# Second maximum and second exponentials moved directly behind the first, and a block's layer-norm steps behind the maxima

## What is computed

```python
def attention(x, w_kv_down, w_kv_up, w_q, w_out):
    kv = (x @ w_kv_down) @ w_kv_up
    k, v = kv[..., :HD], kv[..., HD:]                 # 16 heads of 64
    q = x @ w_q
    att = einsum('bqhd,bkhd->bhqk', q, k) * 64 ** -0.5
    att = softmax(where(causal, att, -inf), axis=-1)
    return einsum('bhqk,bkhd->bqhd', att, v).reshape(B, T, HD) @ w_out

def ffn(x, centroids, gamma, beta, W1, b1, W2, b2):
    expert = argmax(feats @ centroids.T, axis=1)
    alpha = sigmoid(sum(feats * centroids[expert], axis=-1))
    h = layernorm(feats) * gamma[e] + beta[e]
    y = feats + relu(h @ W1[e].T + b1[e]) @ W2[e].T + b2[e]     # e = expert of the token
    return alpha * y + (1 - alpha) * feats

x = x + layernorm(attention(layernorm(x)))
x = x + layernorm(ffn(layernorm(x)))
```

## Time and profile before

| | us |
|---|---|
| timed runs, median (lowest to highest) | 1460.65 (1459.31 to 1461.14) |
| the profiled execution, its own time | 1459.58 |
| span of its trace | 1457.7 |
| TensorE / VectorE / ScalarE / GpSimd busy, share of the span | 92% / 85% / 74% / 56% |
| the attention's steady part, 30 to 1235 us: TensorE busy | 1146.59 of 1205 |
| one iteration (16 slots) in the steady part | 75.88 |
| mean granted TensorE clock (1 is full) | 0.977 |

### The profile page before, as it was taken

How to read it: one execution, slowest core, us unless ns; L and a number is a source line. 1 busy time by engine, 2 the same in 40 slices (tenths; PEclk the granted TensorE clock), 3 DMA queues, 4 the chain that set the end, 5 groups by cost and what they waited for, 6 DMA issues and landing times.

```text
span 1457.7 us, 34718 instructions
## 1 busy us (share of the span) xinstructions
PE 1343.0 (92%) x9120; PEld 1210.6 (83%) x9120; DVE 1234.4 (85%) x4806; ACT 1083.2 (74%) x3186; POOL 809.8 (56%) x1216
## 2 busy tenths in 40 slices
PE   7999999999999999999999999999999999599993
PEld 6988898888888988888888888888888888488872
DVE  5899888888888888888888888888888887499994
ACT  5888787878787878788787878787878886366661
POOL 3445555555555555555555555555555554178886
PEclk9999999999999999999999999999999999699997
DMA  4000000000000000000000000000000000312120
GB/s 194 5 9 12 12 11 12 11 8 11 12 11 12 11 11 10 9 11 11 11 11 12 11 10 11 10 11 12 11 12 11 9 9 14 95 48 63 59 62 8
DMA packets 38793, 32.39 MB, mean 22 GB/s; under 512 B 4882, under 2 KB 35990, under 8 KB 38304
## 3 DMA queue, kind: packets, MB, share of 16 engines
q1 hardware_dynamic: 31968, 21.61, 4.9%
q0 software_dynamic: 4608, 8.67, 1.7%
q10 hardware_dynamic: 2112, 1.11, 0.3%
HBM read 20.35 MB, written 12.07 MB: 22 GB/s over the span
## 4 chain that ended last, share of the span: by engine, by line
DVE 46%; issue 22%; ACT 18%; POOL 6%; PE 5%; ACTq 1%; DMA 1%; DVEq 1%; POOLq 0%; SPq 0%
DVE nscore L851 15%; DVE p_lo L861 13%; ACT prob L722 10%; ACT t_hi L694 5%; DVE nmax L851 2%; POOL prob L1037 2%; DVE ff L367 2%; DVE hitr L891 2%; DVE wup_s L384 1%; DVE on L393 1%; POOL pay L1056 1%; DVE fn L793 1%; DVE gg L402 1%; DVE t_lo L838 1%; DVE rinv L832 1%
## 5 line engine op out<-in xcount | busy, mean ns | idle before, releaser
L1037 POOL TENSOR_TENSOR prob<-prob,rinv 128x256 f32<-128x256 f32 (+1 forms) x512 | 413.2, 828 | 507.8 <-DVE rinv L832 507.7
L722 ACT ACTIVATE prob<-nscore,nmax 128x128 f32<-128x128 f32 (+1 forms) x1024 | 458.7, 449 | 248.4 <-DVE nmax L851 248.4
L851 DVE CUSTOM_DVE_ANT_0 nscore<-psS,mask 128x128 f32<-128x128 f32 (+1 forms) x1024 | 319.9, 350 | 0.0
L861 DVE TENSOR_TENSOR p_lo<-psP,p_hi 128x768 fp32r<-128x768 f32 x256 | 243.7, 952 | 1.0 <-ACT p_hi L694 0.9
L838 DVE TENSOR_TENSOR t_lo<-psT,t_hi 128x512 fp32r<-128x512 f32 x256 | 175.9, 687 | 56.0 <-ACT t_hi L694 56.0
L607 PE MATMUL psP<-ident,prob 128*128 128x128 f32 x1536 | 216.4, 277 | 6.8 <-DVE p_lo L861 6.7
L694 ACT ACTIVATE p_hi<-psP 128x768 fp32r<-128x768 f32 x256 | 204.9, 800 | 1.6 <-PE psP L607 1.6
L579 PE MATMUL psS<-t_lo,xt_hi 128*128 128x256 f32 (+1 forms) x512 | 196.8, 384 | 0.0
L722 ACT ACTIVATION_READ_ACCUMULATOR prob<-nscore,nmax 128x1 f32 x1024 | 191.3, 187 | 0.0
L607 PEld LDWEIGHTS psP<-ident,prob 128*128 128x128 f32 x1536 | 167.2, 141 | 22.7 <-POOL prob L1037 8.8
L867 DVE TENSOR_TENSOR z_lo<-psZU,z_hi 128x512 fp32r<-128x512 f32 x256 | 175.7, 686 | 3.3 <-ACT z_hi L694 3.3
(11 more groups left out here) (167 smaller groups left out, 3246.0 us busy)
## 6 DMA issues: line engine op xcount, KB each, us to landing
fin<-routed_rows SPq DMA_DIRECT2D x40, 136.0 KB, 2.2
wx<-ffn_w SPq DMA_DIRECT2D x2, 2058.0 KB, 12.0
xin<-x SPq DMA_DIRECT2D x32, 128.0 KB, 2.1
xres<-x SPq DMA_DIRECT2D x32, 128.0 KB, 2.1
out<-res,fin POOLq DMA_INDIRECT x80, 2.3
routed_rows<-padr ACTq DMA_DIRECT2D x4, 272.0 KB, 4.3
routed_rows<-padr SPq DMA_DIRECT2D x4, 272.0 KB, 5.4
wup_s<-wup SPq DMA_DIRECT2D x1, 1024.0 KB, 4.9
```

The costliest lines, as they stand in the source:

```text
L722: last = nc.scalar.activation(prob[:, p1, h, a:z], nscore[:, h, a:z], ACT.Exp, bias=nmax[:, p1, h, q:q + 1], scale=-1.0, accum_out=rsum[:, ...
L851: last = v.tensor_tensor_reduce(nscore[:, h, a:z], psQ[q][:, h, :], mask[:, a:z], -1.0, -MASKED, ALU.add, ALU.min, nmax[:, p1, h, q:q + 1])
L861: v.tensor_tensor(p_lo[:, (s - 3) % 2], psP[:, :, 0:384], p_hi[:, (s - 3) % 2].bitcast(F32), ALU.subtract).then_inc(S["p_split"], 1)
L1037: last = g.tensor_tensor(pr, pr, rinv[:, p2, :, q:q + 1].broadcast_to([P, 2, z - a]), ALU.mult)
```

## The change

Three things move; no arithmetic is added or taken away.

1. On VectorE `score_max(1)` stands directly behind `score_max(0)` and ahead of `p_lo` (in r = 4 the routing's step 3 stays between them, its step 4 follows them). On ScalarE `exps(1)` stands directly behind `exps(0)` and ahead of `z_hi`.
2. The layer-norm steps of r = 0 to 3 leave the head of the slot. `block_norms` (`an`; `st3`; `fn` and `st1`; the writes and `xn`) stands behind both maxima and ahead of `p_lo`; `block_moments` (`mv3`, `mv1`) stands between `p_lo` and `z_lo`.
3. On GpSimd the chain of six linked steps in r = 1 is cut: the two that make the reciprocal deviation stay in r = 1 (with two semaphores of their own, `ve3_done` and `rs3_done`, on which `fn` waits), the other four move to r = 2, behind that slot's product with `rinv`.

```diff
             # ScalarE
                 if live(1):
                     exps(0)
+                    exps(1)
                 if live(4):
...
                     cp(z_hi[:, (s - 4) % 2], psZ[:]).then_inc(S["z_hi_done"], 1)
-                if live(1):
-                    exps(1)
             # VectorE
                 if live(1):
                     score_max(0)
                 route(b0, s, live_b, 3)
+                if live(1):
+                    score_max(1)
                 route(b0, s, live_b, 4)
+                block_norms(b0, s, live_b)
                 if live(3):
                     dve.wait_ge(S["p_hi_done"], g0 + s - 2)
                     v.tensor_tensor(p_lo[:, (s - 3) % 2], psP[:, :, 0:384], p_hi[:, (s - 3) % 2].bitcast(F32),
                                     ALU.subtract).then_inc(S["p_split"], 1)
-                if live(1):
-                    score_max(1)
+                block_moments(b0, s, live_b)
                 if live(4):
                     dve.wait_ge(S["z_hi_done"], g0 + s - 3)
...
-            def misc_stats(b0, s, live_b):
+            def block_moments(b0, s, live_b):
...
                 if r == 1 and live_b(2):
                     aggregate(st3, mv3, S["st3_done"], S["mv3_done"], b0 + db - 1)
                 if r == 2 and live_b(-1):
                     aggregate(st1, mv1, S["st1_done"], S["mv1_done"], b0 + db + 2)
+
+            def misc_stats(b0, s, live_b):
...
                 if r == 2 and live_b(2):
-                    n = b0 + db - 1
-                    dve.wait_ge(S["r3_steps"], 6 * n - 4)
+                    dve.wait_ge(S["rs3_done"], n)
                     normalise(lambda t: fn[:, t, :], lambda t: pay[:, db, t, 0:P], mv3,
                               lambda t: pay[:, db, t, C_RSTD:C_RSTD + 1], S["f_ready"])
             # GpSimd
                 if r == 1 and live_b(2):
+                    inv_sqrt(pay[:, db, :, C_RSTD], ve3, mv3[:, :, 1], S["mv3_done"], S["ve3_done"], S["rs3_done"],
+                             b0 + db - 1)
+                if r == 2 and live_b(2):
                     n = b0 + db - 2
-                    k = [6 * n]
+                    k = [4 * n]
...
-                    pool.wait_ge(S["mv3_done"], n + 1)
-                    link(g.tensor_tensor(ve3[:], mv3[:, :, 1], eps_t[:], ALU.add))
-                    link(g.tensor_tensor(rs3, ve3[:], neg_half[:], ALU.pow))
-
+                    pool.wait_ge(S["rs3_done"], n + 1)
                     link(g.tensor_tensor(w3[:, 0, :], mv3[:, :, 1], rs3, ALU.mult))
```

More of the change, by code:

```diff
@@ L149, in block_kernel @@
             bias_done bias_added weights_ready
-            x_loaded xr_loaded st1_done mv1_done ve1_done rs1_done xn_ready xk_hi_done xn_tr xt_hi_done x_split xk_split
+            x_loaded xr_loaded ve3_done rs3_done st1_done mv1_done ve1_done rs1_done xn_ready xk_hi_done xn_tr xt_hi_done x_split xk_split
             t_ready t_hi_done t_split s_ready nmax_ready probs_ready rinv_ready norm_ready pt_ready p_hi_done p_split
@@ L925, in misc_stats, with block_norms @@
                     aggregate(st1, mv1, S["st1_done"], S["mv1_done"], b0 + db + 2)
+            def misc_stats(b0, s, live_b):
+                r, db = s % PAIRS, s // PAIRS
                 if r == 7 and live_b(1):
                     aggregate(st2, mv2, S["st2_done"], S["mv2_done"], b0 + db)
-            def misc(g0, b0, s, live, live_b):
+            def block_norms(b0, s, live_b):
                 r, db = s % PAIRS, s // PAIRS
+                n = b0 + db - 1
                 if r == 0 and live_b(2):
-                    n = b0 + db - 1
                     dve.wait_ge(S["rs2_done"], n)
@@ L962, in misc @@
                     prep_norm((db + 1) % 2, b0 + db + 2, b0 + db + 1)
+            def misc(g0, b0, s, live, live_b):
+                r, db = s % PAIRS, s // PAIRS
+                if not live(0) and s == 9:
+                    dve.wait_ge(S["bias_done"], E // 2 + 1)
+                    b1v = wx[:, :, B1:W2]
+                    v.tensor_tensor(b1v, psT[:, 0, 0:E * FB].rearrange("p (e j) -> p e j", e=E), b1v,
+                                    ALU.add).then_inc(S["bias_added"], 1)
                 if r == 6 and live_b(-1):
```

## The result

The changed kernel takes 1491.39 us (median of four runs, 1490.78 to 1493.51), against 1459.98 for the kernel before beside it: a ratio of 1.0215, with a 95% interval of 1.0199 to 1.0232, or 31.4 us slower. The forecast was slower, but by 9, and its range ended at 1479.

What follows compares the result with a forecast made beforehand. It took a 4.31 us slot cycle through two engines as the bound, TensorE close behind at 4.23. Blocks -5.6, boundary +5.3 and clock +9.6 summed to +9.3 on 1459.58, or 1470.0 on the median; range 1457 to 1479.

Steps and rivals of the forecast that it cites:

- plain slots: Attention slots without extra steps: the new cycle through `z_lo` was to take 4.22 us in place of 4.31.
- the straight line through two points: Loop boundary: TensorE waits of 1.1 us never drop the clock, 2.09 did in 4 of 13; 2.99 gives 8 of 13.
- the block walk: One block of eight slots, r = 0 to 7, summed to 36.79 us against 36.97; over 31 blocks -5.6 us.
- five small routing steps: Slot r = 5, from `z_lo` to first maximum: 1.63 us with these steps, against 1.30 plain.
- rival (c): GpSimd's product with `rinv` holds the moved `fn` and `xn`: 8.4 us; 1469 without the clock, 1478 with it; chance 0.10.
- the slots of r = 5 to 7: Sign that the forecast is right: these slots longer than before, and slot 4 shorter by 0.6 us.
- The boundary, +5.3: Loop's branch: 2.35 us in a cycle without spare time, where it cost 1.94; 13 times 0.41.
- The clock, +9.6: TensorE idling at the boundary: 8 falls to half clock at 1.45 us each, in place of 4 at 0.5.
- My upper bound on the price, 1.7: Clock fall behind a boundary: 3.4 us at half clock loses at most 1.7 us of work; 1.45 was taken.
- Part 3, at nothing: GpSimd's cut chain in r = 1 and 2: product (1.61 us) and moved steps (about 2.5) fill a slot; costed at nothing.

## Why the prediction failed

**The direction and three of the mechanisms were right.** The second exponentials follow the first; `z_lo` waits for `z_hi`; plain slots take 4.19 (forecast 4.22); `z_lo` to the first instruction behind the branch takes 2.99 (2.95). The clock falls behind 8 of 13 boundaries, which is the number given, and an iteration with one stretch is 1.3 to 1.4 longer than without (1.45 given). The products added at the boundary show that it is the falls that cost this, and that without TensorE's idling there they don't come. The number itself owes something to luck: the straight line through two points that gave it is not what the other runs show, with eight boundaries also at 6.7 to 7.0, and six at 7.3 to 7.4.

**The step that failed is the block walk, -5.6 us, measured +10.2.** Most of it, 11.2, is the cast: I priced the "five small routing steps" of r = 5 at their times from the kernel before, where GpSimd's product had ended when the cast came. The change doesn't move it among VectorE's instructions, so it was in no list of moved steps; but it comes 1.32 behind `rinv` in place of 1.85, and the product runs from 0.24 to 1.85 behind `rinv`. I had weighed that hold, but as rival (c) for `fn` and `xn` alone. These two were not held. GpSimd and VectorE in r = 2 of the changed kernel:

```profile
329.69 1.61 POOL L1045 TENSOR_TENSOR prob<-prob,rinv 128x256 f32<-128x256 f32 x2
```

```profile
331.33 0.60 DVE L792 TENSOR_SCALAR fn<-pay,mv 128x128 f32<-128x128 f32 x2
```

`fn` starts 0.03 us behind the product's end and takes its 0.60, as in the earlier trace rows. So these rows say nothing on whether the product could hold it. The mechanism was right and the instruction was not. The Trainium skill (SBUF — State Buffer, Who interferes with whom) lists a cast among the operations that can take the port shared with GpSimd, and says that a tensor_tensor with both inputs in SBUF contends with GpSimd's reads; the rows of the cast (0.56 against 0.16) and of `hitr` (0.81 against 0.175) agree with both.

The other 4.6 are in the walk itself: without the held cast the block takes 36.94 and not 36.79. The walk reaches the first maximum of r = 4 after 18.59, and measured are 18.78; behind that, the cast left out, it is 0.05 too long. The kernel with `an` behind `p_lo` puts 0.3 us a block on `an` ahead of `p_lo`, in r = 1 and 2. I had taken it on the path once, and let TensorE's pace cover it from then on; one block walked once from r = 0 can't show what a late start leaves in the next slots. That the slots of r = 5 to 7 would be longer than before was right for r = 6 (4.87 for 4.31), right for r = 5 by the held cast alone (4.89 for 4.65, and 4.52 with the cast late), and wrong for r = 7 (4.18 for 4.31).

**The boundary, +5.3, measured +7.0.** The place and the mechanism were as given; 2.48 for 2.35.

**The clock, +9.6, measured +12.9 in the twelve iterations, and 14.3 with the fall behind them.** The count was right; the price was not, since four of the eight boundaries have two stretches in a row, at 2.7 us. My upper bound on the price, 1.7, excluded that. The doubled stretches went when `an` was late, which brings the transposes nearer, but also when the cast was late, which leaves the boundary as it is; why, no run shows.

**Part 3, at nothing**: no run takes GpSimd's chain back alone, so that is not shown; in the changed kernel VectorE waits 1.6 us in all for that chain, ahead of `fn`, and 1.7 before.

**What stays open.** Why some boundaries fall and others don't, in one kernel with the same waits: no row that I read tells them apart. And why the late cast takes the second stretches away.

## What to carry to other kernels

When an edit moves VectorE steps, or only shifts in time those that it leaves in place, lay each small one, down to a cast of two elements, beside GpSimd's instructions of the same slot: what a held step costs is the rest of GpSimd's instruction, not its own time, and moving it to where GpSimd is idle can be worth more than the reordering (43 us here, with two 128x16 steps and TensorE's wait behind them). Opening one cycle of hand-overs between engines closes another; before trading, find what stands idle in the old one, because it counts in full in the new. And where TensorE waits at a loop's boundary, look at the granted clock behind it: a few products that nobody reads, put in the wait, gave 12 us back.

## What the runs showed of the hardware

- A VectorE cast of 128x2 from SBUF to SBUF takes 0.16 us, and 0.56 when it meets GpSimd's product, whose end it waits for; `hitr` (128x16, two inputs in SBUF) 0.175, and up to 0.97 in the changed kernel; `oh` (128x16, both inputs in SBUF as well) 0.175, and 0.61 in the kernel before beside GpSimd's split. The maxima from PSUM ran beside the same product at their usual 0.28 and 0.42, and so did the reduction `dstf` (128x2 from 128x16, one input in SBUF) at its 0.16.
- TensorE idling for 0.95 to 1.2 us and then for 1.73, with 1.0 us of work between, was followed by half clock (1.2 in place of 2.4 GHz) behind 8 of 13 boundaries, in four of them for 6.8 us. Where the transposes were 5.7 to 6.1 us apart, or the waits filled with products, there was none.
- At the branch VectorE idles 2.3 to 2.4 us in every kernel here, whichever instruction is the first behind it. The Trainium skill (Runtime: NRT & Kernel Launch, Instruction fetch mechanics) says that a taken branch whose target is not in the pages already fetched forces a fetch before execution goes on; no run here shows that this is the cause.
